# Merged query-key weights, folded normalisations and rewritten queue orders in the first attention of a gated cross-attention and mixture-of-experts kernel

## What is computed

```python
x = x + tanh(g_xattn[0]) * L0_xattn(layernorm(x), ctx, ctx, Wq, bq, Wk, bk, Wv, bv)
x = x + tanh(g_ffn[0])   * L0_ffn(layernorm(x), gate_w, expert_bias, w1, w2)
x = x + tanh(g_xattn[1]) * L1_xattn(layernorm(x), ctx, ctx, ...)
x = x + tanh(g_ffn[1])   * L1_ffn(layernorm(x), weight, bias)
# L0_xattn: one head of width 256, no scale
scores = (q @ Wq + bq) @ (k @ Wk + bk).T ;  out = softmax(scores) @ (v @ Wv + bv)
# L0_ffn: logits over 12 experts (8 real, 4 pass x through), the top 2, softmax of the two
logits = x @ gate_w.T + expert_bias
```

## Time and profile before

| | us |
|---|---|
| Median of 3 runs | 379.73 (379.67 to 382.23) |
| Profiled execution, its own time | 378.42 |
| Its span | 376.6 |
| PE busy | 346.2 (92%) |
| DVE busy | 261.1 (69%) |
| ACT busy | 218.7 (58%) |
| POOL busy | 159.7 (42%) |

### The profile page before, as it was taken

The page is one execution under the profiler, slowest core; times in us unless marked ns, Lnnn a source line. Parts: engine busy times, 40 slices in busy tenths (PEclk is TensorE's granted clock), DMA queues, the critical chain, the costliest instruction groups (busy, mean ns, idle before and its releaser), DMA issues.

```text
span 376.6 us, 9201 instructions
## 1 busy us (share of the span) xinstructions
PE 346.2 (92%) x3030; PEld 278.0 (74%) x3031; DVE 261.1 (69%) x671; ACT 218.7 (58%) x455; POOL 159.7 (42%) x215
## 2 busy tenths in 40 slices
PE   1999999976899999999999998879999999999995
PEld 0888787754799999999999994556676667666674
DVE  1569879895655665654454447878789988967696
ACT  1697899521454454455445442465867787775586
POOL 7497599505355655655555444412130231101100
PEclk9999999999999999999999999999999999999999
DMA  6999762301223333323232214310110000000005
GB/s 188 321 414 394 289 247 84 115 2 56 65 89 114 122 97 129 108 70 81 73 83 70 70 44 132 135 58 2 58 58 24 35 2 2 3 3 2 0 30 195
DMA packets 15386, 38.25 MB, mean 102 GB/s; under 512 B 3574, under 2 KB 4748, under 8 KB 13820
## 3 DMA queue, kind: packets, MB, share of 16 engines
q1 hardware_dynamic: 9978, 22.55, 17.1%
q0 software_dynamic: 3936, 10.45, 9.5%
q10 hardware_dynamic: 1442, 4.85, 3.3%
HBM read 24.34 MB, written 13.50 MB: 100 GB/s over the span
## 4 chain that ended last, share of the span: by engine, by line
PE 76%; DVE 8%; ACT 7%; DMA 3%; issue 3%; POOL 1%; ACTq 1%; DVEq 0%; POOLq 0%
PE two L1717 15%; PE two L1730 14%; PE two L1866 5%; PE two L1749 4%; PE two L1896 4%; PE two L1931 4%; PE two L1852 4%; PE two L1832 3%; PE two L1740 2%; PE two L1578 2%; PE two L1543 2%; PE two L1923 2%; PE two L1558 2%; PE two L1912 1%; DMA kmask<-in_c_head 1%
## 5 line engine op out<-in xcount | busy, mean ns | idle before, releaser
L1207 DVE SCALAR_TENSOR_TENSOR gate<-th,two 128x512 f32<-128x512 f32 x39 | 26.8, 688 | 58.1 <-ACT th L739 32.4
L739 ACT ACTIVATE th<-two 128x512 f32<-128x512 f32 x39 | 23.4, 599 | 70.8 <-PE two L1730 43.4
L546 POOL DMA_INDIRECT y_d<-y_sb,goal_i x39 | 38.6, 989 | 50.5 <-ACT y_sb L749 50.5
L540 POOL DMA_INDIRECT xg<-xn_d,slot_i x39 | 38.0, 974 | 31.2 <-DVE slot_i L1160 13.8
L1717 PE MATMUL two<-wh,gh 128*128 x156 | 44.2, 283 | 0.1
L1717 PE MATMUL two<-wh,gl 128*128 x156 | 44.0, 282 | 0.0
L1717 PE MATMUL two<-wl,gh 128*128 x156 | 43.8, 281 | 0.0
L560 POOL TENSOR_TENSOR rstd<-var,half 128x2 f32<-128x2 f32 x14 | 9.8, 703 | 76.7 <-DVE var L1274 76.7
L1307 DVE TENSOR_REDUCE nm<-two 128x8 f32<-128x960 f32 x32 | 36.1, 1153 | 4.5 <-PE two L1852 4.1
L513 POOL TENSOR_TENSOR wl<-wl,wh 128x512 fp32r<-128x512 f32 x28 | 35.3, 1280 | 6.5 <-ACT wh L668 6.3
L1730 PE MATMUL two<-wh,xh 128*128 x78 | 34.2, 438 | 1.3 <-DVE xl L1201 1.3
(11 more groups left out here) (274 smaller groups left out, 885.7 us busy)
## 6 DMA issues: line engine op xcount, KB each, us to landing
wl<-in_wmoe SPq DMA_DIRECT2D x8, 1024.0 KB, 14.9
y_d<-wh ACTq DMA_DIRECT2D x4, 1024.0 KB
yg<-y_d SPq DMA_DIRECT2D x7, 512.0 KB, 3.4
xn_d<-xq SPq DMA_DIRECT2D x8, 256.0 KB, 2.0
xz<-xn_d SPq DMA_DIRECT2D x8, 256.0 KB
out_x<-of SPq DMA_DIRECT2D x8, 256.0 KB, 2.0
x_sb<-in_x SPq DMA_DIRECT2D x1, 1024.0 KB, 9.6
x_sb<-in_x SPq DMA_DIRECT2D x1, 768.0 KB, 4.7
```

Of the source, the lines that this page charges most:

```text
L540: pool.indirect_dma_start(xg[:, n % 2, :], None, xn_d, bass.IndirectOffsetOnAxis(ap=slot_i[:, n:n + 1], axis=0)).then_inc(gathered[n % 2], 16)
L546: pool.indirect_dma_start(y_d, bass.IndirectOffsetOnAxis(ap=goal_i[:, n:n + 1], axis=0), y_sb[:, n % 2, :], None).then_inc(y_stored[n % 2] ...
L739: nc.scalar.activation(th[:], bank[2 + k][:], ACT.Tanh, scale=0.5).then_inc(th_ok, 1)
L1207: dve.scalar_tensor_tensor(gate[:, k, :], th[:], 1.0, bank[2 + k][:], ALU.add, ALU.mult).then_inc(gate_ok, 1)
```

## The change

- The keys are no longer projected batch by batch. `Wk` is transposed on TensorE, multiplied by `Wq` once into `merged` (128 by 256), and six products of 480 columns give the merged keys of all batches. The bias terms come from eight products of one column.
- The first normalisation goes. Subtracting the mean of a row is the same as subtracting the mean of `Wq` over its input rows, which VectorE does once (`sum_queries`, `centre_queries`). TensorE transposes the raw x. The division is folded into the exponential: `scale=rstd0`. The bias row is spread over the rows by a diagonal matrix of the standard deviations (`spread_std` on ScalarE, two per batch), in a float32 product of 128 rows per tile. The negated maximum is multiplied by rstd on VectorE, a second instruction in `max0_of`, both of whose inputs are in SBUF.
- The second normalisation is taken out of the gate in the same way: the gate weights are centred once, TensorE transposes the raw x1, and `logits_of` multiplies by rstd1 and adds the bias, in two instructions per batch instead of one. `norm1` stays for the rows that are stored.
- `xq1` has four buffers instead of two. `copy_xT1` of batches 3 to 7 is ScalarE's. `xT` of all batches lies in the room of the last high weights, so `high` of chunk 20 and later waits for the last scores.
- The clearing DMAs are SyncE's, ahead of the weight loads 6 and 7.
- The queues of TensorE, ScalarE, VectorE and GpSimd are written out by hand. VectorE does 3 `low` instead of 4, GpSimd 29 instead of 28, of which 8 stand behind its last `root1`. The projections of the second attention move behind the last gate product, and TensorE gets more filling products (`busy`).

```diff
+            def sum_queries():
+                dve.wait_ge(wq_in, 32)
+                own.mark(dve.tensor_reduce(wsum[:], wq0_sb[:], AX, ALU.add))
+                own.settle()
+                own.mark(dve.tensor_scalar(wless[:], wsum[:], -1.0 / D, None, ALU.mult))
...
             def max0_of(b):
                 dve.wait_ge(scores_done, b + 1)
                 wait(dve, exp_done, b - 1)
-                dve.tensor_reduce(negmax[:, b % 2, :], bank[6][:, 0:U * LK].rearrange("p (u k) -> p u k", u=U), AX,
-                                  ALU.max, negate=True).then_inc(max_done, 1)
+                own.mark(dve.tensor_reduce(lowest[:, b % 2, :], bank[6 + b % 2][:, 0:U * LK].rearrange("p (u k) -> p u k", u=U), AX,
+                                           ALU.max, negate=True))
+                own.settle()
+                dve.tensor_tensor(negmax[:, b % 2, :], lowest[:, b % 2, :], rstd0[:, b, :], ALU.mult).then_inc(max_done, 1)
...
             def logits_of(b):
...
+                for u in range(U):
+                    ins = dve.scalar_tensor_tensor(logit[:, cols(2 * b + u, E_ALL)], gate_bank(b)[:, u * GATES:u * GATES + E_ALL],
+                                                   rstd1[:, b, u:u + 1], gbias_sb[:, cols(u, E_ALL)], ALU.mult, ALU.add)
...
+            def spread_std(b):
...
+                for u in range(U):
+                    ins = nc.scalar.activation(spread0[:, b % 2, u, :], ident[:], ACT.Copy, scale=std0[:, b, u:u + 1])
...
+            def keys_by_query(n):
+                m, h = KEYS[n]
...
+                w = merged[:, m * P:(m + 1) * P] if m < C else biases[:, C:C + 1].to_broadcast([P, P])
+                pe.matmul(keys_bank(n), w, ctxT_sb[:, h * HB:(h + 1) * HB], start=True, stop=True,
+                          skip_group_check=True).then_inc(kq_done, 1)
...
             def scores0(b):
+                for u in range(U):
+                    dst = bank[6 + b % 2][:, u * LK:(u + 1) * LK]
+                    pe.matmul(dst, spread0[:, b % 2, u, :], kq[:, b, cols(C, LK)], start=True, stop=False,
+                              skip_group_check=True)
                     for c in range(C):
...
@@ the end of GpSimd's list
+            root1(4)
+            low(20)
+            root1(5)
+            low(21)
+            root1(6)
+            low(23)
+            root1(7)
+            for j in range(24, 32):
+                low(j)
             pool.wait_ge(slots_kept, 1)
...
@@ VectorE's list, the middle and the end
+            max0_of(6)
+            stats1(3)
+            add_x1(4)
+            max0_of(7)
+            copy_v0(6)
+            logits_of(1)
+            stats1(4)
+            low(14)
+            add_x1(5)
+            logits_of(2)
+            stats1(5)
+            low(22)
...
+            logits_of(5)
+            dve.wait_ge(logit_kept, EARLY // U)
+            highest(0, lg, 0, EARLY)
+            stats1(7)
+            mark_highest(0, lg, 0, EARLY)
+            logits_of(6)
+            keep_first(0, 0, EARLY)
+            leave(0, EARLY)
+            highest(1, left, 0, EARLY)
+            logits_of(7)
...
@@ ScalarE's list, the end
+            copy_xT1(6)
+            copy_xT1(7)
+            for j in range(26, 28):
+                high(j)
+            norm1(5)
+            for j in range(28, 31):
+                high(j)
+            norm1(6)
+            norm1(7)
+            high(31)
```

More of the change, by code:

```diff
@@ L45 @@
 NB = 4
+NX = 4
 HG = HEADS // NB
@@ L614, in _, with copy_wkT @@
             act.dma_start(bv0_sb[:], bv0.partition_broadcast(P)).then_inc(wv_in, 16)
[L615 to L624, removed]
-                ins.then_inc(kt_ok, 1)
+            def copy_wkT():
+                act.wait_ge(merge_pe, WKT)
+                nc.scalar.activation(wkT[:].rearrange("p c n -> p (c n)"), bank[0][:, 0:D], ACT.Copy).then_inc(merge_act, 1)
@@ L705, in _ @@
-            for j in pieces:
-                high(j)
+            copy_xT(0)
+            copy_wkT()
+            gains_of()
+            copy_merged()
+            copy_keys(0)
+            copy_keys(1)
+            spread_std(0)
+            copy_xT(1)
+            spread_std(1)
+            copy_keys(2)
+            copy_keys(3)
+            high(0)
+            copy_xT(2)
+            copy_keys(4)
+            spread_std(2)
+            for j in range(1, 3):
+                high(j)
+            exp0_of(0)
@@ new lines, in _ @@
+            copy_keys(5)
+            high(3)
+            copy_probT(0)
+            high(4)
+            exp0_of(1)
+            high(5)
+            spread_std(3)
+            copy_xT(3)
+            exp0_of(2)
+            copy_probT(1)
+            copy_xT(4)
+            for j in range(6, 8):
+                high(j)
+            spread_std(4)
+            high(8)
+            copy_xT(5)
+            high(9)
+            copy_probT(2)
+            copy_xT(6)
+            exp0_of(3)
+            high(10)
@@ new lines, in _ @@
+            norm1(0)
+            for j in range(11, 13):
+                high(j)
+            copy_probT(3)
+            copy_xT(7)
+            spread_std(5)
+            for j in range(13, 15):
+                high(j)
+            exp0_of(4)
+            spread_std(6)
+            high(15)
+            copy_probT(4)
+            exp0_of(5)
+            high(16)
+            spread_std(7)
+            high(17)
+            norm1(1)
+            copy_probT(5)
+            for j in range(18, 21):
+                high(j)
@@ new lines, in _ @@
+            exp0_of(6)
+            high(21)
+            exp0_of(7)
+            copy_probT(6)
+            copy_xT1(3)
+            norm1(2)
+            for j in range(22, 24):
+                high(j)
+            copy_xT1(4)
+            norm1(3)
+            copy_probT(7)
+            high(24)
+            copy_xT1(5)
+            norm1(4)
+            high(25)
+            copy_xT1(6)
+            copy_xT1(7)
+            for j in range(26, 28):
+                high(j)
+            norm1(5)
@@ L1695, in _ @@
                     busy(bank[5], 1)
+            products1(10, len(P1))
             def experts(i):
```

587 lines of the change are left out of this document (350 added, 237 removed).

## The result

The changed kernel ran in 376.57 us (median of 11, 375.78 to 378.71), the kernel before beside it in 380.58 (median of 11, 379.28 to 382.37). The ratio is 0.9909, with a 95% interval of 0.9887 to 0.993: faster by 0.9%, some 3.5 us by the ratio and 4.0 between the medians, where I had forecast 380.2 and no change. It is at the edge of what I had called measurable, and the interval leaves "no change" out. The profiled executions differ by less, 374.6 against a span of 376.6, because the one shown of the kernel before is an execution in which TensorE's granted clock never fell (1.000), while over its executions beside these runs the time goes from about 378.5 to 383 us as the mean clock goes from 1.000 to 0.98.

What follows compares the result with a forecast made beforehand. PE was taken as nearly full from 9 to 73 us, other engines with little room. T = 63.8 plus 22.0 put G, the first gather, at 85.8 against 85.36, +0.4: 380.2 us from 379.73; 8-in-10 range 370 to 384.5.

Steps and rivals of the forecast that it cites:

- The mechanism: VectorE beside GpSimd: a short operation with two SBUF inputs waits for the whole `low` under way, about 1.25 us.
- rival B: Routing chain and stage one: no blocking to speak of; T = 59.8, G = 74.8, time 369.2; chance 0.18.
- G: Instant of the first gather, 85.36 us in the kernel before, forecast 85.8; what it loses, the span loses.
- Rival C: Operations meet the `low` half as often; T = 61.8, G = T + 18.5 = 80.3, time 374.7; chance 0.12.
- T: End of `stats1(7)` on VectorE, the mark for stage one's end; forecast 63.8 us, between 60.6 and 66.8.
- T to G: Routing chain up to the first gather: 11.75 to the last `low`'s end plus 10.26, so 22.0 us.
- the idle share: VectorE's idle part of stage one: 16% taken, against 23% in the kernel before, since PE no longer fills the loop.
- the blocked time: VectorE in stage one: 3.4 us of waiting in the new multiplication and three `low`, eleven operations, bounds 0 and 13.8.
- Rival D: Stage one: blocks also delay ACT and PE, VectorE idles 23%; T = 68.4, G = 90.4, time 384.7; chance 0.20.
- The projections of the second attention fill PE while it waits: TensorE between the last gate product and the gather: moved projections only fill waiting time; no cost was given.
- ScalarE's sum: ScalarE's work in stage one: 15.4 us removed, 15.1 added, so no change; clearing DMAs priced separately at 0 to 2.
- Late weights: Loads 6 and 7 behind the clearing DMAs: even 15 us later, chunks arrive before `high(24)` at about 55 us.

Runs made afterwards that it cites:

- e1: Changed kernel with one operand of each marking operation of the routing chain put into PSUM, small copies added; ratio to the kernel before 0.976.
- e2: Changed kernel with GpSimd's last eight `low` done on 16 of 512 columns, leaving the rest of those low parts out; ratio to the kernel before 0.9731.
- b1: Kernel before with eight instead of three `low` behind GpSimd's last root, nothing left out; ratio to the kernel before 1.0082.
- e9: Changed kernel with the maximum of the scores in PSUM and ten unused products where TensorE waited in the last batches; ratio to the kernel before 0.9906.
- e4: Changed kernel with the maximum of the scores written to PSUM, the new multiplication's first input; no fillers added; ratio to the kernel before 0.9922.
- e11: Changed kernel with the second attention's eight value products moved from around the one-hot groups to behind the rank products, filling products adjusted; ratio to the kernel before 0.9877.
- e8: Changed kernel with 28 instead of 8 filling products behind the last key product; ratio to the kernel before 0.991.
- e6: Changed kernel with routing operands, maximum, row counts and places in PSUM, value products behind the ranks, four fillers instead of twelve; ratio to the kernel before 0.9809.
- e3: Changed kernel with 2 instead of 12 filling products between the ranks and the list of slots; ratio to the kernel before 0.9963.
- e7: Changed kernel with the five clearing DMAs issued by ScalarE behind its first `norm1` instead of by SyncE; ratio to the kernel before 0.9893.
- e10: Changed kernel with routing operands and maximum in PSUM, value products behind the ranks, fillers in the last batches and behind the slot products; ratio to the kernel before 0.9716.

## Why the prediction was wrong, by its own steps

**The mechanism was right.** An operation with two SBUF inputs is locked out for a whole `low`; the eight `low` behind the last root slow the routing chain to one such operation per `low`. I expected `hot`, `left`, `eq` and `cand` at 1.0 to 1.3 (0.98 to 1.48 measured), a median near 0.2 and a most above 1 for the multiplication (0.221 and 1.099). E1, e2 and b1 show it from three sides, and rival B (no blocking) is out, since G would have been at 74.8. Rival C (half the meetings) is out for the routing chain, where it had 18.5 from T to G; for stage one it was the better count, since five of the eleven operations met a `low`. The Trainium skill's page SBUF — State Buffer, section "SBUF: two separate sides", calls the pair of ports an exclusive lock with one side fully blocked; e1's 1.22 against 0.30 agrees with it.

**The step that failed is T.** I had 14.2 + 41.7 / 0.84 = 63.8, with bounds of 60.6 and 66.8, and measured 59.73, which is 4.1 less and below the bounds. The start (14.28) and VectorE's work (38.0 against 38.3) were right. Two terms were mis-sized: the idle share, which I took as 16% and which is 12% (5.46 of 45.53 us), worth 2.2 (41.7 / 0.88 = 47.4, T = 61.6); and the blocked time, 3.4 taken, 2.1 measured (1.87 in the multiplication and 0.2 in one `low`), worth 1.9 with the 0.3 of work (40.07 / 0.88 = 45.5). That I divided the blocked time by 0.84, so that 1 us of it costs 1.19, is not borne out either: in e9 1.0 us less of it shortened the stage by 0.64. Why the idle share was 12% is not shown. TensorE's load bears on it, since at half clock (e4) VectorE idles more, but no run changes that share alone. T came out where rival B had it (59.8), by other terms, so T by itself would not have told the two apart. Rival D, with an idle share of 23%, fell with the same number.

**T to G was 23.28 instead of 22.0**, by two errors of opposite sign. The end of the second `eq` came 11.26 behind T instead of 11.75 (-0.5). From there to G I took 10.26 from the earlier trace rows as untouched, and it was 12.02 (+1.8). "The projections of the second attention fill PE while it waits" is the sentence that failed: eight of them stand around and between the one-hot groups, where TensorE doesn't wait and VectorE waits for it. e11 gives 1.5 for them, e8 0.2 for the clock.

**The sum.** 85.8 - 4.1 - 0.5 + 1.8 = 83.0, the measured G. Behind it the span is 291.59 instead of 291.24. In terms of the kernel before, stage one gained 5.9 us (T from 65.67 to 59.73) where I had forecast 1.9, and 3.6 of it was paid back between T and G (19.69 to 23.28) where I had 2.3. The expected gain of stage one was there; I had made it too small. In medians, the 3.6 us between 380.2 and 376.57 are 2.8 for G, less 0.35 behind it, and 1.2 for a term that I took over unread: the median lay 1.3 above the profiled execution in the kernel before, whose profile happened to be of an execution with a clock of 1.000, and only 0.1 above it in the kernel after.

**Further steps.** ScalarE's sum is nothing: right. TensorE loses about 8 us: 6.5 in the window, which holds new fillers. Late weights: ScalarE's `high` (L726) didn't wait, where it had waited 0.5, and the loads landed in 14.1 us (14.9 in the earlier trace rows), with the clearing DMAs ahead of two of them. Right, as the group and the DMA row of the kernel after show:

```profile
L726 ACT ACTIVATE wh<-wl 128x512 fp32r<-128x512 f32 x32 | 19.1, 628 | 0.0
```

```profile
wl<-in_wmoe SPq DMA_DIRECT2D x8, 1024.0 KB, 14.1
```

That the gather alone tells the span: right by 0.35 as long as the clock holds. What the prediction doesn't have at all is the clock in the stages behind the change, below.

## What to carry to other kernels

Before a list of GpSimd instructions is put ahead of a chain of short VectorE operations, count the VectorE operations with two SBUF inputs: each cost up to one GpSimd instruction here, at 16 columns as at 192, and one of its operands in a free corner of PSUM took the cost away (here 4.2 us for a few small copies). Then look where the blocking went: with one operation freed, the next one with two SBUF inputs can meet the `low` instead (`pairs` in e1, VectorE's own `low` in e9, where half of the 1.87 us came back). And in a pipeline with idle time only part of what is really taken out reaches the end (here 0.64 of 1.0), so don't divide blocked time by a busy share. When something is moved to "where TensorE waits", ask between which two instructions of the other engine's chain it will stand.

## What the runs showed that I had not expected

A gain can come back as a lower clock. After a stretch in which TensorE was less busy, its granted clock fell to 0.50, and what this cost went with who set the pace behind it: 0.2 us in the routing chain (e8), 1.8 in the last batches (e4 against e9), and in the first experts products of 0.63 us instead of 0.40 (e6). In the table the span from G to the end is 291.2 to 291.8 in all seven profiles in which the clock held from G to about 368 us, and 292.8 to 293.8 in the seven where it fell (e3 to e7, e11, b1), so a fall there costs 1.2 to 2.5 us. Removing work or waits ahead of it can cause one (e4, e6), and so can removing fillers (e3): the mean clock of these three was 0.986 or less in every one of their executions, where that of e1, e2 and e10 was 0.995 or more. For the others a fall belongs to the execution as much as to the kernel. The kernel before ran with mean clocks from 1.000 down to 0.979, and e11, whose profile has a fall at 86 us, had 1.000 in three of its six. One profile doesn't tell which; the clocks of the other executions do.
